# Attention's weighted sums in groups of 512 queries in place of 256

## What is computed

```python
Q = (x @ WQ + bQ).reshape(b, s, h, dh).transpose(0, 2, 1, 3)     # K and V alike
scores = jnp.einsum('bhqd,bhkd->bhqk', Q, K) / scale
scores = jnp.where(causal, scores, jnp.float32(-100000.0))
A = jax.nn.softmax(scores, axis=-1)
Z = jnp.einsum('bhqk,bhkd->bhqd', A, V)
out = jnp.einsum('bhsd,de->bse', Z, WO) + jnp.float32(h) * bO
```

## Time and profile before

| | us |
|---|---|
| median of 3 runs | 1577.11 (1573.95 to 1580.8) |
| the profiled execution | 1581.26 |
| its span, first to last instruction | 1579.5 |
| attention, from the first score to the last weighted sum | 565.1 to 1120.8 |

### The profile page before, as it was taken

The page is one execution under the profiler, slowest core; times in us unless marked ns, Lnnn a source line. Parts: engine busy times, 40 slices in busy tenths (PEclk is TensorE's granted clock), DMA queues, the critical chain, the costliest instruction groups (busy, mean ns, idle before and its releaser), DMA issues. The chain is left out here.

```text
span 1579.5 us, 32613 instructions
## 1 busy us (share of the span) xinstructions
PE 1429.2 (90%) x10020; PEld 978.9 (62%) x10020; DVE 1029.0 (65%) x2383; ACT 775.6 (49%) x1316; POOL 636.5 (40%) x676
## 2 busy tenths in 40 slices
PE   4899999999968879999999999999598999999997
PEld 3777888888846623443444344443276778888886
DVE  5675536365779678877788687784267564445557
ACT  4313565555125514665566466567362245655530
POOL 3371433766634460222222122222235406176764
PEclk9899999999979968999999999999879999999999
DMA  7741656887316910432224242200131227488873
GB/s 258 231 191 54 195 184 203 264 244 241 87 58 169 239 62 2 69 54 43 42 42 68 34 64 42 42 2 2 41 96 69 97 64 245 154 264 249 245 224 107
DMA packets 159219, 199.06 MB, mean 126 GB/s; under 512 B 18181, under 2 KB 132441, under 8 KB 159065
## 3 DMA queue, kind: packets, MB, share of 16 engines
q1 hardware_dynamic: 140632, 146.67, 34.9%
q0 software_dynamic: 18432, 50.36, 9.7%
HBM read 105.21 MB, written 91.49 MB: 125 GB/s over the span
## 5 line engine op out<-in xcount | busy, mean ns | idle before, releaser
L1576 ACT ACTIVATE attn_prob<-attn_b_ps 128x1024 f32<-128x1024 f32 (+3 forms) x352 | 304.1, 870 | 219.6 <-PE attn_b_ps L1744 217.7
L1622 DVE TENSOR_REDUCE attn_max_a<-attn_a_ps 128x1 f32<-128x512 f32 (+3 forms) x432 | 279.1, 669 | 72.5 <-PE attn_a_ps L1727 40.5
L475 POOL DMA_INDIRECT xs_dram<-ffn_xn,ffn_index x192 | 189.0, 984 | 229.1 <-DVE ffn_index L745 172.8
L1724 PE MATMUL attn_a_ps<-k_rows,q_rows 96*128 96x512 bf16 (+3 forms) x768 | 250.1, 348 | 21.2 <-DVEq L1614 7.5
L489 POOL DMA_INDIRECT ffn_gathered<-ys_dram,ffn_index x192 | 195.8, 1020 | 92.8 <-issue 56.0
L1520 POOL TENSOR_SCALAR_AFFINE_SELECT attn_prob<-attn_prob 128x512 f32<-128x512 f32 x128 | 81.3, 636 | 363.5 <-ACT attn_prob L1576 360.7
L789 DVE TENSOR_TENSOR ffn_xs_lo<-ffn_xt_ps,ffn_xs_hi 128x512 fp32r<-128x512 f32 x144 | 97.7, 679 | 160.1 <-ACT ffn_xs_hi L561 159.6
L1768 PE MATMUL attn_o_ps<-attn_prob,attn_v_now 128*17 128x256 f32 (+1 forms) x2560 | 187.8, 366 | 0.0
L1744 PE MATMUL attn_b_ps<-q_rows,k_rows 98*128 98x512 bf16 (+3 forms) x768 | 186.2, 330 | 0.3 <-ACT attn_prob L1576 0.3
L1724 PEld LDWEIGHTS attn_a_ps<-k_rows,q_rows 96*128 96x128 bf16 x768 | 75.0, 98 | 180.0 <-DVE attn_max_a L1622 103.2
L186 PE MATMUL ffn_gu_ps<-ffn_w_hi,ffn_xs_hi 128*128 x564 | 170.7, 303 | 2.1 <-DVE ffn_xs_lo L789 2.1
(11 more groups left out here) (196 smaller groups left out, 2691.7 us busy)
## 6 DMA issues: line engine op xcount, KB each, us to landing
ffn_xs<-xs_dram SPq DMA_DIRECT2D x138, 256.0 KB, 3.4
ys_dram<-ffn_y SPq DMA_DIRECT2D x138, 256.0 KB, 2.5
xs_dram<-ffn_y SPq DMA_DIRECT2D x16, 768.0 KB, 11.7
qk_parts<-proj_cut SPq DMA_DIRECT2D x32, 384.0 KB, 3.1
k_rows<-qk_parts SPq DMA_DIRECT2D x96, 128.0 KB, 4.5
q_rows<-qk_parts SPq DMA_DIRECT2D x96, 128.0 KB, 6.5
ffn_w_stage<-in_L_ffn_w_dram SPq DMA_DIRECT2D x64, 128.0 KB, 2.4
x_res<-in_L_attn_x_dram SPq DMA_DIRECT2D x4, 1024.0 KB, 8.3
```

The lines of the kernel that those rows point to most:

```text
L475: pool.indirect_dma_start(xs_dram[(b + 1) % 2], bass.IndirectOffsetOnAxis(index[:, b, i, k:k + 1], 0), xn[:, b % 2, i, :], None, bounds_ch ...
L1576: act.activation(prob[PROB[kt]][:, h:h + heads, prob_at(kt, kt * P):prob_at(kt, S)], b_ps[:, slot, :].rearrange("p (h t) -> p h t", h=head ...
L1622: dve.tensor_reduce(dst, a_ps[:, bank, 0:heads * keys].rearrange("p (h k) -> p h k", h=heads), AX.X, ALU.max).then_inc(a_free, 1)
L1724: ins = pe.matmul(a_ps[:, bank, i * keys:end], q_rows[q][0:SROWS, h0 + i, qt * P:(qt + 1) * P], k_rows[q][0:SROWS, h0 + i, first:first + k ...
```

## The change

The queries of a group are cut at 512, one PSUM bank of `o_ps`, in place of 256. A key tile has one or two parts in place of one to four. The parts cut to the causal range are 512 + 512, 512 + 384, 512 + 256, 512 + 128, 512, 384, 256 and 128 columns for key tiles 0 to 7. Of two old places the later one stays; the last place of each tile is what it was. The flag that starts a sum is now set by both halves of tile 0, each in its own bank.

```diff
-        QUARTER = HALF // 2
-
-        def quarters(kt):
-
-            qs = list(range(kt * P // QUARTER, S // QUARTER))
-            return qs[1:] + qs[:1]
-
-
-        WEIGH = [(6, 7, 8, 9), (10, 11, 12, 13), (14, 15, 16), (17, 18, 19), (20, 21), (22, 23), (24,), (25,)]
+        def halves(kt):
+
+            hs = list(range(kt * P // HALF, S // HALF))
+            return hs[1:] + hs[:1]
+
+
+        WEIGH = [(7, 9), (11, 13), (14, 16), (17, 19), (21,), (23,), (24,), (25,)]
...
-                    quarter = quarters(kt)[places.index(n)]
-                    at, end = max(quarter * QUARTER, kt * P), (quarter + 1) * QUARTER
+                    half = halves(kt)[places.index(n)]
+                    at, end = max(half * HALF, kt * P), (half + 1) * HALF
...
-                                        start=(kt == 0 and quarter in (1, 2)),
-                                        stop=(kt == (at // HALF + 1) * HALF // P - 1))
+                                        start=(kt == 0),
+                                        stop=(kt == (half + 1) * HALF // P - 1))
```

## The result

The changed kernel takes 1581.93 us in the median of 16 runs (1576.14 to 1586.63), the kernel before 1575.52 (16 runs). The ratio is 1.0044, with a 95% interval from 1.0029 to 1.006: slower by 7 us, between 4.6 and 9.5 (the medians differ by 6.4). That is within the half per cent that the forecast called no measurable change, and within its range, but the sixteen runs do tell it from zero.

The account below looks back on a forecast made before the run. PE was taken to set the pace, DVE next. Fourteen units at +0.04 us (+0.6) and -1.4 at the end gave -0.8; against the runs' median of 1577.11 the forecast was 1576 us, range 10 us down and 15 up.

Parts of the forecast that it names:

- What bounds the kernel: Attention loop: PE sets the pace, busy 122 of 123 us; DVE is next at 99, ACT has 80.
- The one stall of a unit: Behind step 4 of a unit (one batch, four heads), a query-major score waits 0.34 us for DVE.
- What the change removes: Weighted sums: 12 groups a unit in place of 20, saving 1.84 us a unit, 29 us over 16.
- The piece of 0.23: Fixed cost of a weighted-sum group in us: 0.14 within the group and 0.09 at the mask matmul ahead.
- What it moves: Steps losing their group no longer cover PE's wait for a bank: stalls of 1.88 us against 1.84 saved.
- the walk: Step-by-step comparison, per new light step, of PE's distance between two bank uses with what a use needs; stalls sum to 1.88.
- The sum: Whole kernel: 14 units at +0.04 us give +0.6, the last units -1.4, together -0.8; forecast 1576 us.
- come whole: First rival: with slack in PE's ring the new stalls stay away and 29 us are saved, 1548 us; chance 0.13.
- the ring: Two PSUM banks PE and DVE share for query-major scores; one use to the next takes 1.17 us, masked 1.23.
- the second rival: DVE stays behind, light steps stall twice: +2.2 us a unit, 1608 us; chance 0.22, shared with costly 512 groups.
- The clock: Third rival: PE's granted clock falls in the loop; a tenth at 1.2 GHz adds some 50 us; chance 0.03.
- The likeliest case: No measurable change: an error of 0.4 us a unit either way stays inside 8 us; chance 0.62.

Follow-up runs that it names:

- e1: The changed kernel with DVE's row maxima taken over only the first half of each bank's keys: 1555.28 us, ratio 0.9846.
- e2: The kernel before with DVE's row maxima taken over only the first half of each bank's keys: 1571.32 us, ratio 0.9962.
- e6: The kernel before with only key tile 0's sums in groups of 512, all others in 256 at their old places: 1571.94 us, ratio 0.9968.
- e3: The changed kernel with each wide group issued as two of 256 queries in a row, at the same late places: 1584.6 us, ratio 1.0042.
- e5: The kernel before, groups of 256, with another table of query-major banks per step: 1583.11 us, ratio 1.0029.
- second pair of profiles: Both kernels run once more, unedited, for a second profile of each: changed 1580.5 us, before 1577.38 us.
- e4: The changed kernel with another table of query-major banks, one for most steps without a group, two or three with: 1558.13 us, ratio 0.9874.

## Why the prediction was wrong, point by point

**What bounds the kernel.** Right: PE before, and DVE behind it; e1 and e2 show how near behind. One reading was wrong. The one stall of a unit was taken for a cost of DVE's; e2 shows that without it PE waits as long for ACT.

**What the change removes.** Right in kind, a little high: 1.84 us a unit was forecast and 1.75 measured. A group of 512 holds PE 0.98 us, as taken. The piece of 0.23 came from times with two digits; what remains is 1.75 / 8 = 0.22, and e6 measures (31.47 - 31.07 + 0.06) / 2 = 0.23. Within a group eight rows more cost 0.01 us (0.99 and 0.98 in e3). The rule of the Trainium skill (TensorE: Matmul & The Clock Gate, Back-to-back issue gap), 2.5 ns per matmul, makes that 0.02, an estimate from the page, which is near; it leaves out the change of kind between scores and sums. The Trainium skill (TensorEngine Tiling (Array Packing), Key Properties) has such a cost, without a figure: a change of tiling mode drains TensorE. The weighted sums, 17 columns wide and 32 partitions apart, differ in this from the scores, and 0.22 us a round trip does not contradict it; that the drain is the cause was not tested by itself.

The trace of the kernel before has another candidate, the weight loads:

```profile
767.53 0.10 PEld L1724 LDWEIGHTS attn_a_ps<-k_rows,q_rows 96*128 96x128 bf16 x1
...
768.06 0.13 PEld L1768 LDWEIGHTS attn_o_ps<-attn_prob,attn_v_now 128*17 128x17 f32 x8 [0.21 <-issue]
768.62 0.10 PEld L1724 LDWEIGHTS attn_a_ps<-k_rows,q_rows 96*128 96x128 bf16 x1 [0.42 <-DVE attn_max_a L1622]
```

Among scores a load runs ahead of its matmul: that of 767.53 is for a score that starts at 767.75. At a group and behind it the load starts only with its matmul, at 768.06 and 768.62. So the 0.22 us can as well be two loads of 0.10 that no matmul covers; no run tells this from a drain. A third candidate, the change from bf16 to f32 by itself, falls by a place of e5, where f32 transposes of 128 columns follow a bf16 mask after 0.06 us, as a bf16 score does:

```profile
841.58 0.22 PE L1727 MATMUL attn_a_ps<-mask_qk,ident_b 128*128 128x128 bf16 x1
841.64 1.04 PE L1788 MATMUL attn_b_ps<-ident,attn_o_sb 128*128 128x128 f32 x8
```

**What it moves.** This is the step that failed. The mechanism, the place of each stall and most sizes were right: seven stalls forecast, seven found, each within 0.03. But the sum was 1.88 against 2.22, and the forecast hung on the difference between it and the saving. Behind step 15 the walk stopped at the first stall and left DVE without a backlog, but the four narrow scores at its end had just kept both banks in use, so that step 16 stalls for a bank once more, 0.08 (823.48 to 823.99, where 0.43 would do). The walk also left out that DVE joins the maxima at this place, which costs 0.09 (824.31 to 824.96, where a group of 256 takes 0.56). That is 0.17 in all. The wait of 0.06 for the exponential behind step 6 was passed over with "ACT has the room". The rest, 0.11, is differences of up to 0.03 a stall, none of them to the other side.

**The sum.** +0.04 us a unit was forecast, +0.47 measured: over the 14 units with query-major scores 6.6 us where 0.6 stood. At the end, behind the last query-major score, -1.4 was forecast, and from the transposes of the third unit from the end to the last weighted sum (1073.75 to 1120.53 before, 1079.55 to 1123.76 after) the changed kernel is faster by 2.6 us; the second pair of profiles gives 1.1. That leaves some 4 to 5.5 us, which is what the traces show, at the lower end of the runs' interval. The period of 31.94 lies above the 31.4 to 31.8 that the forecast named as its sign, and below the 32.1 that would have refuted it.

**The rivals.** The saving did not come whole: the ring was there. It did not become the bound in the sense of the second rival either, since 2.22 stays under the 2.4 named there. The price given there for a 512 group at twice a 256, +1.9 a unit, takes the whole saving as lost; the 0.09 ahead of each of eight groups would have stayed, which makes it 1.88 - 0.72 = +1.2. The clock kept at 1.00 in the stretch read above. The likeliest case carried 0.62, and by its own bound of half a per cent it is what happened; what was wrong is the number zero inside it. The forecast took the difference of two sums of some 1.9 us each, each off by a tenth or more, and multiplied it by 14. Its range, 15 us up, left room for that; the sum itself did not, though everything that a walk passes over is a stall and so leans to the slower side.

## What to carry to other kernels

A group of work on the bounding engine may also be the cover under which another engine returns a buffer. Before spreading such groups more coarsely, lay the distance between two uses of each buffer against what one use takes, step by step, with what the step before leaves over and with everything else that the returning engine has to do there (the join at step 16); then move the work that uses the buffers to the steps that keep their cover (e4), rather than only merging the groups. And a stall that stands alone in a periodic time line need not cost anything: see whether a later wait of the same period would take its place.

## What was not expected of the hardware

Two f32 groups of 256 columns in a row cost TensorE what one of 512 does (0.99 and 0.98 us), so the 0.22 us of a group belong to the change between 128-column bf16 scores and 17-column f32 sums, not to the instructions. And a maximum of half the columns shortened a bank's absence from 1.23 to 0.97 us, by 0.26, close to the 0.27 by which its row got shorter: the rest of the way, from PE's issue to DVE's start and from DVE's end to PE, stays as it is.
